# A graph network kernel: one-hot products for three more chunks of layers 1 to 3, and a third buffer for the words from which the one-hot matrices are built

## The reference

```
def _genconv(h, edge_attr, src, dst, w1, b1, g1, bb1, w2, b2, t):
    msg = relu(h[src] + edge_attr) + EPS_MSG
    m = msg * t
    seg_max = segment_max(m, dst, num_segments=N)
    ex = exp(m - seg_max[dst])
    denom = segment_sum(ex, dst, num_segments=N)
    alpha = ex / (denom[dst] + 1e-16)
    agg = segment_sum(msg * alpha, dst, num_segments=N)
    out = h + agg
    z = relu(_layernorm(out @ w1 + b1, g1, bb1))
    return z @ w2 + b2
# layer 0: h = x @ enc_node_w + enc_node_b ; e = edge_attr @ enc_edge_w + enc_edge_b
# layers 1 to 3: z = relu(_layernorm(h, ...)); h = h + _genconv(z, e, ...)
```

## Time and profile before

| | us |
|---|---|
| median of 3 runs | 3556.5 |
| lowest and highest | 3553.41 and 3565.63 |
| the profiled execution's own time | 3565.84 |
| its span in the profile | 3564.0 |

### The profile page before, as it was taken

One profiled execution on the slowest core, in us unless ns is written; L12 is line 12 of the kernel. 1 busy time (PEld: TensorE's weight loads), 2 busy tenths in 40 slices (PEclk: granted clock), 3 DMA queues, 4 the chain that ended last, 5 costly groups with the idle time before them and its releaser, 6 DMA issues.

```text
span 3564.0 us, 49979 instructions
## 1 busy us (share of the span) xinstructions
PE 2685.9 (75%) x19276; PEld 1379.9 (39%) x19276; DVE 2861.8 (80%) x2825; ACT 1771.3 (50%) x2228; POOL 2401.5 (67%) x2477
## 2 busy tenths in 40 slices
PE   3676576766555899989943999999944789998974
PEld 2332232322232444444431444444423444444433
DVE  6798899988955888887875788888885688887986
ACT  3676676665523544454542445554543355444544
POOL 5777676767347777776736777777745777777752
PEclk7787887888757999999956999999965899999985
DMA  5899898988726999999844999999954799999971
GB/s 142 248 275 282 252 286 254 265 252 254 192 64 189 289 296 289 283 289 287 237 99 139 266 288 289 293 297 294 277 123 135 206 282 288 292 295 266 297 185 40
DMA packets 1048366, 853.28 MB, mean 239 GB/s; under 512 B 912954, under 2 KB 938559, under 8 KB 1018368
## 3 DMA queue, kind: packets, MB, share of 16 engines
q1 hardware_dynamic: 940688, 470.61, 52.6%
q10 hardware_dynamic: 27232, 285.62, 21.3%
q0 software_dynamic: 80208, 93.86, 10.6%
HBM read 537.69 MB, written 312.14 MB: 238 GB/s over the span
## 4 chain that ended last, share of the span: by engine, by line
DVE 30%; PE 27%; ACT 10%; SPq 10%; DMA 8%; issue 8%; POOL 7%; DVEq 0%; ACTq 0%; POOLq 0%
PE X L544 21%; SPq L355 7%; DVE decay L903 7%; POOL gath L484 6%; DVE state_all L934 5%; DVE one_hot L998 5%; DVE rows_all L889 4%; DMA keep<-keep_dram 4%; DVE X L908 3%; PE X L525 3%; SPq L345 3%; DMA between<-bits_dram 3%; DVE state_all L918 2%; ACT X L656 2%; ACT msg L654 2%
## 5 line engine op out<-in xcount | busy, mean ns | idle before, releaser
L484 POOL DMA_INDIRECT gath<-z_table,idx x2344 | 2278.0, 972 | 941.6 <-issue 710.7
L544 PE MATMUL X<-one_hot,z_parts 128*64 128x512 fp8e5 x10200 | 1194.8, 396 | 226.4 <-DVE one_hot L998 226.4
L544 PEld LDWEIGHTS X<-one_hot,z_parts 128*64 128x64 bf16 x10200 | 587.6, 114 | 881.8 <-DVE one_hot L998 265.6
L544 PE MATMUL X<-between,z_parts 128*64 128x512 fp8e5 x6300 | 699.8, 381 | 0.0
L525 PE MATMUL X<-attr,enc_edge 128*128 128x512 f32 x824 | 480.5, 712 | 257.3 <-DVE state_all L934 249.7
L666 ACT ACTIVATE decay<-X 128x1024 f32<-128x1024 f32 (+2 forms) x216 | 209.2, 968 | 903.3 <-DVE X L908 786.9
L918 DVE TENSOR_TENSOR_SCAN state_all<-decay,state_all,X 128x1024 f32<-128x1024 f32 (+2 forms) x216 | 468.5, 2169 | 91.3 <-ACT X L671 91.3
L889 DVE STREAM_TRANSPOSE rows_all<-state_all 128x1024 f32<-128x1024 f32 (+3 forms) x432 | 505.7, 1171 | 7.5
L544 PEld LDWEIGHTS X<-between,z_parts 128*64 128x64 bf16 x6300 | 351.9, 110 | 370.2 <-issue 62.2
L903 DVE TENSOR_TENSOR_SCAN decay<-X,decay 128x1023 f32<-128x1023 f32 (+2 forms) x216 | 477.2, 2209 | 7.9 <-DVE decay L901 0.2
L934 DVE TENSOR_TENSOR_SCAN state_all<-decay,state_all,X 128x1024 f32<-128x1024 f32 (+2 forms) x216 | 468.0, 2167 | 0.0
(11 more groups left out here) (157 smaller groups left out, 1561.2 us busy)
## 6 DMA issues: line engine op xcount, KB each, us to landing
rows_table<-rows_all SPq DMA_DIRECT2D x784, 256.0 KB
attr<-attr_t SPq DMA_DIRECT2D x196, 512.0 KB
one_hot<-one_hot_dram ACTq DMA_DIRECT2D x45, 1920.0 KB
between<-one_hot_dram ACTq DMA_DIRECT2D x42, 1920.0 KB
one_hot<-one_hot_dram ACTq DMA_DIRECT2D x45, 1280.0 KB
one_hot_dram<-one_hot SPq DMA_DIRECT2D x29, 1920.0 KB
between<-one_hot_dram ACTq DMA_DIRECT2D x42, 1280.0 KB
gath<-z_table,idx POOLq DMA_INDIRECT x2344
```

Of the source, the lines that this page charges most:

```text
L484: pool.indirect_dma_start(out=gath[s][:, n * F:(n + 1) * F], out_offset=None, in_=z_table, in_offset=bass.IndirectOffsetOnAxis(ap=idx[:, c ...
L544: last = nc.tensor.matmul(x[h * F:(h + 1) * F, BANK:CH], z_parts[:, i * GB + k, third, :], bank[:, i, k, h * BANK:(h + 1) * BANK], start=F ...
```

## The change

Chunks 9, 25 and 41 are added to `CHOSEN`, so that layers 1 to 3 do one-hot products in 32 chunks instead of 29. `FIRST_CHOSEN` stays: in layer 0 these three are still gathered whole, but their matrices are built and stored there. The words of the matrices get a third buffer, `bits_third`, and the words of bank n + 3 are loaded when bank n is built. The line numbers of what follows it in the file rise by one or two.

```diff
 HOT_SLOTS = 2
+BIT_SLOTS = 3
 FIRST_CHOSEN = [c for c in range(NCH) if c % 2 == 0 and 4 <= c <= 48]
-CHOSEN = [c for c in range(NCH) if (c % 2 == 0 or c % 8 == 5) and 4 <= c <= 48]
+CHOSEN = [c for c in range(NCH) if (c % 2 == 0 or c % 8 == 5 or c % 16 == 9) and 4 <= c <= 48]
...
-        bits_now = [shared[:, 0:N_BITS], between[:, N_SHARED + N_AGG:N_SHARED + N_AGG + N_BITS]]
+        bits_now = [shared[:, 0:N_BITS], between[:, N_SHARED + N_AGG:N_SHARED + N_AGG + N_BITS], sb("bits_third", [P, N_BITS])[:, :]]
...
-                if n >= 2:
-                    sp.wait_ge(built, (n - 1) * PIECES_1H)
-                sp.dma_start(bits_now[n % 2].bitcast(u8).rearrange("p (r c) -> p r c", c=BANK_COLS),
+                if n >= BIT_SLOTS:
+                    sp.wait_ge(built, (n - BIT_SLOTS + 1) * PIECES_1H)
+                sp.dma_start(bits_now[n % BIT_SLOTS].bitcast(u8).rearrange("p (r c) -> p r c", c=BANK_COLS),
...
-            load_bits(1)
+            for n in range(1, BIT_SLOTS):
+                load_bits(n)
...
-                        if n is not None and n + 2 < NB1H:
-                            load_bits(n + 2)
+                        if n is not None and n + BIT_SLOTS < NB1H:
+                            load_bits(n + BIT_SLOTS)
```

More of the change, by code:

```diff
@@ L279, in gnn_kernel @@
         banks_landed, bits_steps, bits_ready, bits_stored = sem("banks_landed"), sem("bits_steps"), sem("bits_ready"), sem("bits_stored")
-        bits_landed, off_lane, spread, built = sems("bits_landed", 2), sem("off_lane"), sem("spread"), sem("built")
+        bits_landed, off_lane, spread, built = sems("bits_landed", BIT_SLOTS), sem("off_lane"), sem("spread"), sem("built")
         used, hot_stored, hot_landed = sem("used"), sems("hot_stored", len(PARTS)), [sems(f"hot_landed{s}_", len(PARTS)) for s in range(HOT_SLOTS)]
@@ L361, in load_bits @@
                     sp.wait_ge(z_split, 1)
-                if n >= 2:
-                    sp.wait_ge(built, (n - 1) * PIECES_1H)
-                sp.dma_start(bits_now[n % 2].bitcast(u8).rearrange("p (r c) -> p r c", c=BANK_COLS),
+                if n >= BIT_SLOTS:
+                    sp.wait_ge(built, (n - BIT_SLOTS + 1) * PIECES_1H)
+                sp.dma_start(bits_now[n % BIT_SLOTS].bitcast(u8).rearrange("p (r c) -> p r c", c=BANK_COLS),
                              bits_dram[:, n * BANK_COLS:(n + 1) * BANK_COLS].unsqueeze(0)
-                             .broadcast_to([P, PIECES_1H + 1, BANK_COLS])).then_inc(bits_landed[n % 2], 16)
+                             .broadcast_to([P, PIECES_1H + 1, BANK_COLS])).then_inc(bits_landed[n % BIT_SLOTS], 16)
             def store_part(n, part):
@@ L674, in spread_lanes @@
                 if ks[0] == 0:
-                    act.wait_ge(bits_landed[n % 2], 16 * (n // 2 + 1))
+                    act.wait_ge(bits_landed[n % BIT_SLOTS], 16 * (n // BIT_SLOTS + 1))
                     if n > 0:
                         act.wait_ge(spread, GB * n)
-                    nc.scalar.activation(lane_miss, lane_bytes[n % 2], ACT.Abs, bias=lane_off[:, :]).then_inc(off_lane, 1)
+                    nc.scalar.activation(lane_miss, lane_bytes[n % BIT_SLOTS], ACT.Abs, bias=lane_off[:, :]).then_inc(off_lane, 1)
                     act.wait_ge(off_lane, n + 1)
@@ L990, in build_part @@
                 if part == 0:
-                    dve.wait_ge(bits_landed[n % 2], 16 * (n // 2 + 1))
+                    dve.wait_ge(bits_landed[n % BIT_SLOTS], 16 * (n // BIT_SLOTS + 1))
                     dve.wait_ge(spread, GB * (n + 1))
@@ L999, in build_part @@
                                     lane_bits[n % 2].rearrange("p (k c) -> p k c", k=GB),
-                                    bits_words[n % 2][:, i * BW:(i + 1) * BW].unsqueeze(1).broadcast_to([P, GB, BW]), ALU.bitwise_and)\
+                                    bits_words[n % BIT_SLOTS][:, i * BW:(i + 1) * BW].unsqueeze(1).broadcast_to([P, GB, BW]), ALU.bitwise_and)\
                         .then_inc(built, 1)
```

## The result

| | before | after |
|---|---|---|
| median of the timed runs, us | 3554.95 | 3650.74 |
| ratio, 95% interval | | 1.0252 (1.0218 to 1.0286) |
| profiled execution, span | 3564.0 | 3649.7 |

One of the four timed runs of the changed kernel took 5837.43 us: it is left out of the ratio and counts in the median, which is 3649.99 us without it.

What follows compares the result with a forecast made beforehand. The DMA engines were taken as full in layers 1 to 3, with PE close behind. 3565.8 + 72 (layers 1 to 3) - 17 (layer 0) = 3621 us profiled, 9.3 above the median: 3611 us, 8 in 10 between 3566 and 3660.

Steps and rivals of the forecast that it cites:

- What bounds the kernel: Layers 1 to 3, chunks 4 to 48: DMA engines at 0.98, PE and POOL nearly full, VectorE not.
- Layers 1 to 3: Added banks lengthen the three changed groups, PE and DMA nearly level: 24 us a layer, +72 us for three.
- The walk at full clock: Changed groups of layers 1 to 3: PE at full clock needs 117.4 us, as used in the faster rival.
- Layer 0: Three more banks cost 11.5 us of DMA each, but the third buffer removes stalls: -17 us in sum.
- The third buffer: Layer 0: words load earlier, removing a stall in the third bank of every run of consecutive ones.
- 34.5 us for three more banks: Layer 0, chunks 4 to 48: full DMA time added to 731 us by building and storing three banks and loading their words.
- the lower bound of 42: Layer 0: every group at DMA share 1.00 with the sum spread evenly, and -13 ahead: -42 us.
- The -8: Layer 0, chunks 4 to 48: taken between -16 at a DMA share of 1.00 and -1 at 0.98.
- Layer 0 gives nothing back: Rival: in layer 0 builds wait for stores of the one `one_hot` tile, +20 us there; 3649 us, chance 0.12.
- The engines have room: Rival: DMA isn't the limit; PE alone holds layers 1 to 3, +37, layer 0 -53; 3541 us, chance 0.10.
- PE keeps its waits: Rival: changed groups of layers 1 to 3 take 16.1 us more each, +145 us; 3684 us, chance 0.12.

Runs made afterwards that it cites:

- E6: E1 with only half of the result-row stores in layers 1 to 3; 3521.59 us, ratio 0.9888.
- E5: E1 with two instead of three bf16 parts of the node table multiplied in layers 1 to 3; 3530.18 us, ratio 0.9903.
- E1: Changed kernel with rows of bits_dram 33 KiB apart instead of 32; 3558.85 us, ratio 1.0018 to the kernel before.
- E2: Changed kernel with the earlier 29 chosen chunks, so only the third buffer is new; 3492.26 us, ratio 0.9819.
- E4: Kernel before the change with rows of bits_dram 32 KiB apart instead of 29; 3626.01 us, ratio 1.0196.
- E8: E2 with a bank's six rows stored behind each other, read as one piece of 6144 bytes; 3500.42 us, ratio 0.9843.
- E9: E1 with rows 40 KiB apart, on another chip; 4686.5 us where the kernel before took 4632.3.

## Why the prediction came out as it did

**What bounds the kernel: right.** The DMA engines were full in layers 1 to 3, and E6 shows that they hold the unchanged groups. That PE and the DMA meet in a changed group was right too, though at 117.9 us of PE's work and 120 of the DMA's (1.01 of 118.8) they lie 2 us apart and not within 1; E5 and E6 show both walls.

**Layers 1 to 3: mechanism right, +72 too large; measured +45 in the trace.** The rows that answer are those of the changed groups: 118.8 us instead of 120 to 122. For PE, 16.1 us were laid on the 104.4 to 105.4 of the earlier trace rows. These hold some products at the lower level, 1.2 GHz (the mean granted is 0.96 to 0.97): behind the wait of 5.38 us in the earlier trace rows the four edge products take 3.75 us. In the changed groups nearly no wait is left, the clock is granted at 1.00, all at 2.4 GHz, the same four products take 1.95 us, and the work is 117.9 us. The only waits of PE in the group from chunk 20 of layer 1:

```profile
1465.12 1.95 PE L527 MATMUL X<-attr,enc_edge 128*128 128x512 f32 x4 [0.46 <-DVE state_all L936]
1524.52 1.96 PE L527 MATMUL X<-attr,enc_edge 128*128 128x512 f32 x4 [0.46 <-DVE state_all L936]
```

The walk at full clock, 117.4, stood only in the rival. For the DMA, 119.8 us of work were right, but the share reads 1.01 to 1.02 where 1.00 was taken as full. By medians E1 and E2, which differ in the three chunks (and in rows 33 instead of 29 KiB apart), lie 67 us apart; in the traces 56 of it are in these stretches (1866 to 1922 us) and 13 in layer 0's.

**Layer 0: the step that failed.** The prediction had: "The words are 0.79 MB ... 3.5 us for a MB, so 2.7 us". It priced the three added loads and took the 29 others as unchanged. The runs show that all 32 got dear, from 54.7 to 95.2 ns a packet, which for the 768 packets of a bank on 16 engines is from 2.6 to 4.6 us, because the number of banks is also the distance between the rows. The prediction added up 765.5 us of full DMA time for chunks 4 to 48 of layer 0; it was 816 (0.96 of 850.2), and 746 in E1. E1 takes the distance away alone (-92 us), E4 puts it in alone (+71 us), so that it is the cause is shown. That the cause behind it lies in how such addresses fall together in memory is an inference. The Trainium skill ("DMA: Bandwidth & Descriptors", Latency and other measured facts) tells of dear row distances that are large powers of two, and of a few KiB of padding as the cure. The direction agrees; the page's distances begin at 512 KiB, while here 32 KiB cost 40 ns a packet and 1 KiB of padding was enough.

**The third buffer: mechanism right, worth too little.** The order of SP said that the stall would go, and it went. The forecast gave layer 0 17 us back, after 34.5 us for three more banks, so 51 for the buffer; E2 measured 62. Layer 0 with all three changes but good rows (E1) is 46 us shorter than before (33.4 and 12.4) instead of 17. That is past even the lower bound of 42 in the text. The -8 for the chunks from 4 to 48 came from the sentence "What is late next is the DMA", by which each group was counted at the DMA's work. E1 undercuts it in the group from chunk 4 (143.8 us, counted as 153.4): three added banks cost 15 to 20 us of DMA time in the traces (731 before, 726 in E2, 746 in E1) instead of 34.5, and what the group takes is POOL's 111.2 us of work and 32.6 us of gaps. POOL's time in layer 0 stands nowhere in the prediction.

**The sum.** By medians: -62 for the third buffer (E2), +67 for the three chunks (E1 against E2), +92 for the rows (after against E1), together +96. Without the last, the forecast of +54 would have been too slow by 50 us. Two errors with opposite signs met, and that the time fell into the range is luck.

**The rivals.** "Layer 0 gives nothing back" had the time, 3649, and its sign, builds that wait for their store, is there (65.5 us). But with good rows these waits don't appear in E1, so its cause, two stores sooner behind each other, isn't the one: they are as close there. "The engines have room" fell for layers 1 to 3: E5 doesn't move the changed groups. For layer 0 it came near: the DMA isn't the wall there either (E8), and E1's stretch lies 24 us above VectorE's 737. "PE keeps its waits" fell: two waits of 0.46 us are left in the group from chunk 20.

## What to carry to other kernels

When a count goes up, look for every stride that is made of it: here three more banks moved the rows of a small table to 32 KiB apart and cost more than the whole rest of the change. Price the transfers that stay, not only the added ones; the mean duration of one size of packet, before and after, showed it here. A DMA share near 1 doesn't yet make the DMA the wall: where it is read at 0.99, look whether another engine works without a stop beside it. And where a change has two parts, time each alone: the third buffer by itself (E2, 3492 us, 1.8% faster than before) is the version to keep.

## What the runs showed of the hardware

Reading 1024 bytes from each of six rows, by all 128 partitions, took 51 to 56 ns a packet with rows 29 or 33 KiB apart, 70 at 48, 81 to 87 at 40, 87 at 64 and 92 to 98 at 32. On two of the chips the kernel before took 4569 and 4632 us instead of 3554. There PE had single products with 0.8 to 1.6 us between them and no wait that the profile shows (656 us in all in E9), while DMA packets of 256 bytes took 22.8 ns instead of 20.7; the cause is open. The DMA share reads up to 1.02 in a window of 119 us, so that a reading of 1.00 doesn't prove that nothing more fits.
